# Four attention layers on one core: normalisation issued apart from the transposes, a quantisation in five pieces, and group transposes issued after the value products

## What is computed

```python
x = x + jnp.tanh(g_xattn[0]) * _L0_xattn_ref(_layernorm(x, axis=-1), ctx_2048, ...)   # 16 heads, 8 wide
x = x + jnp.tanh(g_ffn[0])   * _L0_ffn_ref(_layernorm(x, axis=-1), ...)               # 8 experts with a capacity
x = x + jnp.tanh(g_xattn[1]) * _L1_xattn_ref(_layernorm(x, axis=-1), ctx_2048, ...)   # 8 heads, no projections
x = x + jnp.tanh(g_ffn[1])   * _L1_ffn_ref(_layernorm(x, axis=-1), ...)               # dense
x = x + jnp.tanh(g_xattn[2]) * _L2_xattn_ref(_layernorm(x, axis=-1), ctx_2048, mask, ...)  # scores clipped, a norm on the output
x = x + jnp.tanh(g_ffn[2])   * _L2_ffn_ref(_layernorm(x, axis=-1), ...)               # 16 experts, two per token
x = x + jnp.tanh(g_xattn[3]) * _L3_xattn_ref(_layernorm(x, axis=-1), ctx_2048, ...)   # below
x = x + jnp.tanh(g_ffn[3])   * _L3_ffn_ref(_layernorm(x, axis=-1), ...)               # 4 experts, one per token
```

```python
def _fq_sym(x, axis):
    s = jnp.max(jnp.abs(x), axis=axis, keepdims=True) / 127.0
    s = jnp.maximum(s, 1e-08)
    q = jnp.clip(jnp.round(x / s), -127.0, 127.0) * s
q = (x @ Wq + bq).reshape(1, B * N, H, hd)
q = jnp.transpose(q * scale, (0, 2, 1, 3))        # scale = 0.25
q = _fq_sym(q, axis=-1)
```

## Time and profile before

| | us |
|---|---|
| median of 3 runs (1278.67 to 1281.26) | 1279.09 |
| the profiled execution | 1287.61 |
| its span | 1285.7 |
| PE busy in the span | 969.9 |
| DVE busy | 650.2 |
| ACT busy | 439.9 |
| POOL busy | 383.9 |

### The profile page before, as it was taken

One profiled execution on the slowest core, in us unless ns is written; L12 is line 12 of the kernel. 1 busy time (PEld: TensorE's weight loads), 2 busy tenths in 40 slices (PEclk: granted clock), 3 DMA queues, 4 the chain that ended last, 5 costly groups with the idle time before them and its releaser, 6 DMA issues.

```text
span 1285.7 us, 18945 instructions
## 1 busy us (share of the span) xinstructions
PE 969.9 (75%) x6616; PEld 574.1 (45%) x6616; DVE 650.2 (51%) x1546; ACT 439.9 (34%) x720; POOL 383.9 (30%) x527
## 2 busy tenths in 40 slices
PE   1868787688448889677637981698989999469993
PEld 1434444577314435455424761234444544336662
DVE  1757663335258723256764335787878783301111
ACT  1335545211015521144410430045655667112210
POOL 3213210211375200333304006135555557110002
PEclk9989989688759989878858995569989999679997
DMA  8643641365454200455432663201031000620002
GB/s 191 137 98 90 171 104 62 145 205 170 150 130 123 64 25 0 131 84 98 82 131 77 199 183 94 45 1 38 2 104 35 2 2 2 268 88 25 17 13 74
DMA packets 117820, 117.64 MB, mean 91 GB/s; under 512 B 71848, under 2 KB 107240, under 8 KB 114408
## 3 DMA queue, kind: packets, MB, share of 16 engines
q1 hardware_dynamic: 106496, 95.58, 27.3%
q10 hardware_dynamic: 8160, 12.46, 3.4%
q0 software_dynamic: 3072, 8.39, 2.2%
HBM read 90.53 MB, written 29.62 MB: 93 GB/s over the span
## 4 chain that ended last, share of the span: by engine, by line
PE 48%; DVE 14%; POOL 6%; issue 6%; DMA 4%; ACT 3%; SPq 0%; POOLq 0%; ACTq 0%; DVEq 0%
PE psT L1392 6%; PE psT L1093 6%; PE psB L1093 5%; PE psT L1244 5%; PE psB L1210 4%; PE psO L1288 3%; DVE mxp L1770 3%; PE psB L1406 3%; PE psT L1355 2%; PE psB L1433 2%; PE psB L1457 2%; PE psO L1278 2%; PE psB L1101 1%; POOL scr_sorted L2161 1%; DVE mxp L1774 1%
## 5 line engine op out<-in xcount | busy, mean ns | idle before, releaser
L1770 DVE TENSOR_REDUCE mxp<-psB 128x1 f32<-128x512 f32 x256 | 162.4, 685 | 41.6 <-PE psB L1210 40.5
L1244 PE MATMUL psT<-whole 99*128 99x256 bf16 (+2 forms) x1024 | 156.9, 279 | 11.3 <-issue 10.9
L1774 DVE TENSOR_REDUCE mxp<-psB 128x2 f32<-128x512 f32 x192 | 122.6, 685 | 52.5 <-PE psB L1216 52.4
L1216 PE MATMUL psB<-whole 96*128 96x256 bf16 x384 | 77.8, 315 | 64.3 <-issue 55.0
L1244 PEld LDWEIGHTS psT<-whole 99*128 99x128 bf16 (+2 forms) x1024 | 98.5, 103 | 60.8 <-issue 27.8
L1545 ACT ACTIVATE Pt<-psT,ln 128x1024 f32<-128x1024 f32 x96 | 106.6, 1114 | 54.9 <-PE psT L1244 53.8
L1545 ACT ACTIVATE Pt<-psT 128x1024 f32<-128x1024 f32 x96 | 97.9, 1023 | 73.2 <-PE psT L1244 71.5
L2096 POOL TENSOR_TENSOR rstd<-vare,cst 128x1 f32<-128x1 f32 x64 | 35.6, 559 | 277.8 <-DVE vare L1694 277.6
L1210 PE MATMUL psB<-whole 96*128 96x512 bf16 x256 | 96.6, 434 | 4.2 <-DVE mxp L1770 3.0
L1216 PEld LDWEIGHTS psB<-whole 96*128 96x128 bf16 x384 | 31.4, 107 | 114.2 <-issue 84.4
L1392 PE MATMUL psT<-whole,qf 128*128 x176 | 81.4, 606 | 0.6 <-ACT qf L1594 0.6
(11 more groups left out here) (300 smaller groups left out, 1793.7 us busy)
## 6 DMA issues: line engine op xcount, KB each, us to landing
whole<-in_w SPq DMA_DIRECT2D x32, 512.0 KB, 4.9
whole<-in_w SPq DMA_DIRECT2D x5, 3072.0 KB, 10.2
xn<-scr_sorted ACTq DMA_DIRECT2D x42, 128.0 KB, 2.2
scr_q<-sq SPq DMA_DIRECT2D x48, 96.0 KB, 1.9
scr_k<-sk SPq DMA_DIRECT2D x48, 96.0 KB, 1.9
whole<-scr_k SPq DMA_DIRECT2D x24, 192.0 KB, 3.5
whole<-scr_k SPq DMA_DIRECT2D x72, 64.0 KB, 3.8
whole<-scr_q SPq DMA_DIRECT2D x64, 64.0 KB
```

The costliest lines, as they stand in the source:

```text
L1216: ins = pe.matmul(dst[:, i * 256:(i + 1) * 256], lhsT=q_at[:, h * A.T + s.tc * P:h * A.T + (s.tc + 1) * P], rhs=k_at[:, h * A.T:(h + 1) * ...
L1244: ins = pe.matmul(psT[:, s.n % 2, i * A.T:(i + 1) * A.T], lhsT=k_at[:, h * kw + s.c * P:h * kw + (s.c + 1) * P], rhs=q_at[:, h * A.T:(h + ...
L1770: dve.tensor_reduce(mxp[:, s.un.g % 2, at:at + 1], psB[:, s.n % BANKS, :], AX.X, ALU.max).then_inc(bank_used[s.n % BANKS], 1)
L1774: dve.tensor_reduce(mxp[:, s.un.g % 2, at:at + 2], psB[:, s.n % BANKS, :].rearrange("p (h n) -> p h n", h=2), AX.X, ALU.max).then_inc(bank ...
```

## The change

Three things are changed in the order, and one in what is computed on DVE.

1. Normalising and transposing are two steps in all layers. For the feed-forward part (`turned`) the stream is now `fn`, `xt`, `xl`. For the fronts of layers 2 and 3 it is `fn` and `fx`; in layer 2 `fn` stands at `u - 0.15` and `fx` at `u + 0.1`, in layer 3 the thunks of unit 0 stand close together as before, and those of units 1 to 3 at offsets from 0 to 0.35 (`rest`), where they stood between 0 and 0.079. The store and the packs of layer 3 stand at 0.42 and 0.43 (0.294 and 0.3 before).
2. The quantisation is five steps (`QUANT_PIECES`): maximum; scale and its reciprocal; multiplication; rounding; multiplication back. The factor 0.25 is taken into the second and the third, which makes the third a `scalar_tensor_tensor`, and the separate instruction L1732 is gone. In unit 0 of layer 3 and for the keys the five follow one another.
3. In layer 2 `onorm` of a group is written behind `pv` of the next group instead of ahead of it.

```diff
-    dict(front=0.498, store=0.58, packs=0.683, body=1.604, end=3.227, start=0.084, span=1.053),
-    dict(front=0.077, fronts=[0.0, 0.01, 0.02, 0.03, 0.04, 0.058, 0.06, 0.079], store=0.294, packs=0.3, max=1.011, ...)]
+    dict(front=0.498, fronts=[-0.15, 0.1, 0.25, 0.35, 0.45], store=0.58, packs=0.683, body=1.604, ...),
+    dict(front=0.077, fronts=[0.0, 0.005, 0.01, 0.02, 0.03, 0.04, 0.045, 0.045, 0.045, 0.045, 0.045, 0.058, 0.06, 0.079],
+         rest=[0.0, 0.02, 0.06, 0.08, 0.11, 0.13, 0.15, 0.18, 0.21, 0.24, 0.27, 0.33, 0.34, 0.35], store=0.42, packs=0.43, ...)]
...
-                    if A.layer >= 2:
-                        s = add("fx", A=A, un=r, j=j, xn=xs, m=take("M"))
-                        r.m_x = s.m
-                    else:
-                        add("fn", xn=xs)
-                        r.xn = xs
+                    add("fn", xn=xs)
+                    r.xn = xs
+                    normal[j] = xs
...
+            def fx(j):
+                def f():
+                    r.m_x = add("fx", A=A, un=r, j=j, xn=normal[j], m=take("M")).m
...
-                    if 0 <= k - 1 < len(tiles) and tiles[k - 1][1] == A.NC - 1:
+                    turn = 0 <= k - 1 < len(tiles) and tiles[k - 1][1] == A.NC - 1
+                    if turn and A.layer != 2:
                         onorm(k - 1)
                     if 0 <= k < len(tiles):
                         pv(k)
                         r.o_of[tiles[k][0]] = r.o
+                    if turn and A.layer == 2:
+                        onorm(k - 1)
...
-            return [f, g] if layer != 1 else [f]
+            return [n, f, g] if layer != 1 else [n, f]
...
-                link(dve.tensor_scalar(qs[:, 1, 0:n * H], qs[:, 0, 0:n * H], 1.0 / 127.0, 1e-8, ALU.mult, ALU.max))
+                    link(dve.tensor_scalar(qs[:, 1, 0:n * H], qs[:, 0, 0:n * H], factor / 127.0, 1e-8, ALU.mult, ALU.max))
...
-                    ins = dve.tensor_tensor(o, v, r.to_broadcast([P, 16, H]), ALU.mult)
+                        ins = dve.scalar_tensor_tensor(out=heads(dst, k), in0=heads(src, k), scalar=factor,
+                                                       in1=per_head(2, k), op0=ALU.mult, op1=ALU.mult)
...
-                    if s.s:
-                        link(dve.tensor_scalar(tmp[:, 0:w], tmp[:, 0:w], 0.25, None, ALU.mult))
-                    quantise(tmp[:, 0:w], tmp2[:, 0:w], 16, s.un.A.nb)
+                    quantise(s.j, tmp[:, 0:w], tmp2[:, 0:w], 16, s.un.A.nb, 0.25 if s.s else 1.0)
...
-                elif s.kind in ("fn", "fx", "xt"):
+                elif s.kind == "fn":
                     normalise(s.xn)
```

More of the change, by code:

```diff
@@ L84 @@
 LOADS = 14
+QUANT_PIECES = 5
 SLOTW = 6144
@@ L201, in q @@
             def q():
-                r.i = quant(r, False)
+                for piece in quant(r, False):
+                    piece()
             def kt(m):
@@ L300, in packs @@
                 add("packs", un=r, A=A, done_before=done())
-            out = [fn(j) for j in range(A.nb)]
+            out = [fn(j) for j in range(A.nb)] + ([fx(j) for j in range(A.nb)] if A.layer >= 2 else [])
             if A.layer in (0, 2):
```

77 lines of the change are left out of this document (49 added, 28 removed).

## The result

The changed kernel takes 1277.4 us, the median of 20 runs (1269.9 to 1282.6); the kernel before takes 1281.2 us in 20 runs beside it (1277.0 to 1292.0). The ratio on record, taken over all runs, is 0.995, with a 95% interval of 0.993 to 0.997 (the quotient of the two medians alone is 0.997, that of the means 0.9955). So the change is worth 5 to 6 us, a fifth of the forecast 26.8; it is faster, but the time lies outside the forecast's range of 1238 to 1270. The profiled execution took 1280.8 us, span 1278.9, granted clock 0.863 (before: 1287.61, 1285.7, 0.862).

A forecast was written before the change was run, and what follows sets the result against it. PE's waits for DVE's normalisation (76.5 us) were the pool; DMAs paced layer 0, two loops layer 2, PE layer 3's body. 1.2 + 10.4 + 4.0 + 9.6 + 1.6 = 26.8 us off 1279.1 gave 1252.3 us, range 1238 to 1270.

The forecast's parts named there:

- Layers 0, 1 and the keys: Layer 0's last front loses its 1.20 us wait; other waits stay covered by DMA waits, layer 1 and keys nothing: 1.2 us.
- Layer 2: Units 3 to 7 drop from 13.44 to 11.75 us each, 8.4 us, plus 2 us in units 6 and 7: 10.4 us.
- the pack loop: Layer 2, key copy through POOL's split, store and packs to first `st`, 14.1 us; forecast to bind at 11.75 us per unit.
- a: Layer 2, from a unit's first `st` to the end of the following front's key copy: 13.2 us before, forecast 9.4.
- Start of layer 3: Score tiles start at once, store and packs moving behind the tokens' combining: 5.7 us less 1.7 of new DVE stops, 4.0 us.
- Fronts of units 2 and 3: Layer 3: two 3.88 us quantisation stops and the half clock behind them go, less 2 us of DVE lag: 9.6 us.
- The clock term: Layer 3 fronts: half clock of 2.6 and 5 us behind the stops costs half of 7.6, and 3.8 us goes.
- Later waits: Layer 3: two later transposes waiting 1.20 us or so for `xn` gain 0.8 us each, 1.6 us.
- B: Rival, half gain: packs in layer 2 and DVE's lag in layer 3's fronts take it back; 9.4 us, 1270; chance 0.18.
- E: Rival, nothing: the wait only changes its name, to the packs in layer 2 and DVE in layer 3; 1279; chance 0.07.
- C: Rival, more: PE regains its clock elsewhere too, layer 2 reaching its 10.8 us loop; 37.3 us, 1242; chance 0.16.
- D: Rival, slower: layer 3's spread fronts keep PE at half clock, 40 us lost; 1294; chance 0.04.

The follow-up runs named there:

- both: Changed kernel with layer 2's query split early on POOL and layer 3's POOL split of units 1 to 3 in four separate steps: 1264.0 us, ratio 0.984 to before.
- q_early: Changed kernel; in layer 2 POOL splits the queries ahead of `rstd`, waiting for the query copy alone: 1262.9 us, ratio 0.984 to before.
- only_layer3: Changed kernel with the order of the tokens' and layer 2's parts put back: 1273.7 us, ratio 0.992 to before; repeated, 1282.2 us, 0.996.
- after_again: The changed kernel as it is, measured once more: 1277.8 us, ratio 0.996 to before.
- spread: Changed kernel with POOL's four split instructions for layer 3's units 1 to 3 set apart, store and packs at 0.54: 1267.9 us, ratio 0.987 to before.
- both_wide: Changed kernel with early layer 2 query split, layer 3 POOL split in four steps, quantisation pieces four or five maxima apart: 1267.2 us, ratio 0.983 to before.
- only_tokens: Changed kernel with the order of layers 2 and 3 put back, leaving the tokens' separate normalisation: 1282.8 us, ratio 0.998 to before.

## Why the prediction was wrong, by its own steps

- **Layers 0, 1 and the keys, 1.2 us**: not refuted, not measurable. The end of layer 0 is at 224.5 us on average in five traces of the old order and at 221.8 in twelve of the new, each with a scatter of 4 us and more.
- **Layer 2, 10.4 us forecast, about 1.6 measured. This step failed**, in two terms. The form of the sum was right: PE's loop is 10.80 and 10.81 us, and the pack loop decides, at (a + 14.1) / 2. The first term is a: I took 9.4 us, worked out at the full clock. At the full clock it is 9.5 to 9.9 (`both` and q_early); but in the change, where PE stops once in two units for 2.3 to 3.5 us, the clock is at 0.74 to 0.85 in it and a is 11.0 to 12.0, so that two units take 25.1 to 26.2 us and not 23.5. The second is the base, 13.44 us from the one trace. Over the five distances from the key copy of unit 2 to that of unit 7 I forecast 8.4 us less; they take 65.5, 63.5 and 63.7 us in before, only_layer3 and its repeat, and 61.4 and 62.8 in the change and after_again, some 2 us less. The 2 us for the last two units came in their distances (24.5 to 21.6 us) and were lost ahead of them, where PE waits 2.3 us for the last packs. That the stop brings the half clock fits the traces: with layer 2's part of the change, behind the twelve waits of 2 us or more the clock in a was 0.74 to 0.87, and behind the eleven of 0.3 to 1.9 us it was 1.00 in six and 0.66 to 0.89 in five. It is not shown by an experiment of its own. My own line for being wrong, `st` waiting over 2 us, was met.
- **Start of layer 3, 4.0 us forecast**: right. S falls from 34.1 (33.9 to 34.3) to 30.6 (29.6 to 31.6), 3.5 us. The maxima start at 808.25, a little ahead of the 809 to 810 forecast, 0.64 us behind the first normalisation.
- **Fronts of units 2 and 3, 9.6 us forecast, 0.6 measured. This step failed too**. G is 110.4 in the traces of the old order and 109.8 on average in the nine with the change in layer 3 and POOL's split in one go (F: 137.7 and 136.8). The 3.88 us stops went. Three things took their place. (1) POOL, which I left out: I costed only the DVE side of the move. The split had stood directly behind the stop (880.93 to 884.74 in the trace of before), where TensorE came back at half clock; set among tiles that run at the full rate it holds up the rounding, and then the value products, by 1.2 and 2.3 us. Spreading it gives 3.8 us of G. (2) In five of the nine traces half clock behind the second of these stops, 2.2 us more. (3) DVE's lag: I took 1 us of waits per front, 2 in all; they are 4.0 us for maxima and 0.9 for `On` (spread, both) where before had 1.2, since the pieces are 5.3 us of work for the 4.2, with the lock against POOL missing. With POOL's split spread G is 5.6 us under the old order, and 8.1 with the pieces further apart (both_wide), which R takes back by 0.7. The clock term was right in sum only: half clock stood for 3.4 and 6.8 us and not 2.6 and 5.0, and it costs about a third of its length (2.2 of 6.9) and not half.
- **Later waits, 1.6 us forecast**: R falls by 0.7 us. Half the size. It comes with the tokens' part: R is 85.6 in only_tokens and 86.3 in only_layer3.
- **Sum**: 1.6 + 3.5 + 0.9 (all of F) + 0.7, some 7 us, against 5 to 6 measured; layer 0 can't be told.

Of the rivals B came nearest (half gain, 9.4 us), for its own two reasons, the packs and DVE, but even its bounds for layer 2 (3) and the fronts (3.2) were too high, and it didn't have POOL either. E, in which the waits only change their names, describes layer 2 about as well. C's 10.8 us stand in every second unit only; also where the packs were shortened (q_early) the average was 11.5. D is refuted: the trace of the change has the front of unit 2, with all five pieces, at the full clock.

```profile
862.00:887.00 25.00, 23.07 (x238) 11.25 (x239) 19.63 (x35) 14.60 (x16) 13.01 (x13) 1.00 0.01 2
```

Of what I said the profile would show, the waits for `xn` (35.2 us, not under 30), the even distance of 11.5 to 12.2 us between fronts, and the absence of waits over 1 us between 860 and 960 did not come true either; and my second line for being wrong, a clock below 0.8 in layer 3's fronts, was met once, with 0.77 from 955 to 970.

## What to carry to other kernels

When a step is moved away from a stop, everything that hung on it comes too, on every engine. Write down for each of them what now stands behind it at the full rate; here POOL's four instructions were hidden by the very stop that the change removed, and spreading them as well gave back 3.8 us, 5.9 with the clock. Where two loops of nearly equal length bind a stage, shortening one is worth little (here -2 us, or even +6) and both 11; and work it out at the clock that the stretch has, not at the full one. A gain under 1% needs a stage's length from several traces, since traces of one and the same order here differ by 5 us in layer 2 and by 9 in layer 0. Choose the ends of a stage so that no half clock from elsewhere lies in it: F scatters by 3 us in one order, G by 0.2 once its half clock is known.
